# Grouped-query attention: the stacked, turned and copied keys of one key head shared by the two pairs of query heads that read them

## The reference, cut to what matters

```python
q = (h @ Wq).reshape(b, s, H, HD)        # H = 16 query heads, HD = 16
k = (h @ Wk).reshape(b, s, HKV, HD)      # HKV = 4 key heads
v = (h @ Wv).reshape(b, s, HKV, HD)
q = _apply_rope(q, cos, sin)
k = _apply_rope(k, cos, sin)
k = jnp.repeat(k, H // HKV, axis=2)      # each key head serves 4 query heads
v = jnp.repeat(v, H // HKV, axis=2)
scores = jnp.einsum('bqhd,bkhd->bhqk', q, k) / np.sqrt(HD)
scores = jnp.where(causal, scores, finfo.min)
ctx = jnp.einsum('bhqk,bkhd->bqhd', softmax(scores), v)
```

## Time and profile before

| | |
|---|---|
| Time, median of 3 runs | 3239.17 us (3236.78 to 3246.33) |
| The profiled execution's own time | 3255.24 us |
| Its span | 3253.5 us, mean granted clock of PE 0.956 |
| PE busy in the span | 2867.8 us (88%) |
| DVE, ACT, POOL busy | 2160.3, 1658.5, 1425.3 us |
| The grouped-query stage | from about 1526 to about 2208 us of the span |

### The profile page before, as it was taken

One profiled execution on the slowest core, in us unless ns is written; L12 is line 12 of the kernel. 1 busy time (PEld: TensorE's weight loads), 2 busy tenths in 40 slices (PEclk: granted clock), 3 DMA queues, 4 the chain that ended last, 5 costly groups with the idle time before them and its releaser, 6 DMA issues. The chain is left out here.

```text
span 3253.5 us, 61489 instructions
## 1 busy us (share of the span) xinstructions
PE 2867.8 (88%) x21526; PEld 2294.2 (71%) x21526; DVE 2160.3 (66%) x6229; ACT 1658.5 (51%) x3452; POOL 1425.3 (44%) x2037
## 2 busy tenths in 40 slices
PE   3878789999999999978898898898799999999986
PEld 2555578888888888846666666666578888888864
DVE  3777678678768777756777777766644455454576
ACT  1544444444444444446666666665454555555553
POOL 3577742342333243275656666322222222222377
PEclk8877899999999999989999999999899999999998
DMA  2464567678777777622333333210355556555445
GB/s 79 163 223 177 197 238 304 255 269 313 274 273 279 280 269 276 246 33 56 92 92 105 105 99 103 97 65 22 132 209 200 206 205 225 196 214 200 140 98 124
DMA packets 192070, 580.15 MB, mean 178 GB/s; under 512 B 22856, under 2 KB 144656, under 8 KB 157456
## 3 DMA queue, kind: packets, MB, share of 16 engines
q1 hardware_dynamic: 154896, 525.03, 43.7%
q0 software_dynamic: 36864, 51.14, 7.7%
HBM read 450.14 MB, written 125.96 MB: 177 GB/s over the span
## 5 line engine op out<-in xcount | busy, mean ns | idle before, releaser
L1119 POOL TENSOR_TENSOR al<-t,ah 128x512 fp32r<-128x512 f32 x220 | 285.5, 1298 | 992.2 <-ACT ah L1331 992.2
L572 PE MATMUL bank<-masks_bf,ident_bf 128*128 128x128 bf16 (+1 forms) x2304 | 581.4, 252 | 138.2 <-ACT ksT L1413 45.3
L526 PE MATMUL bank<-xh,gu 128*128 128x256 f32 x3520 | 629.3, 285 | 9.7 <-issue 4.9
L1779 DVE TENSOR_REDUCE st<-bank 128x1 f32<-128x512 f32 (+3 forms) x1024 | 422.9, 481 | 218.7 <-PE bank L579 211.3
L1426 ACT ACTIVATE pt<-bank 128x512 f32<-128x512 f32 (+1 forms) x1152 | 513.2, 539 | 105.7 <-PE bank L582 95.6
L572 PEld LDWEIGHTS bank<-masks_bf,ident_bf 128*128 128x128 bf16 x2304 | 225.6, 98 | 425.4 <-issue 98.8
L526 PEld LDWEIGHTS bank<-xh,gu 128*128 128x128 f32 x3520 | 506.0, 191 | 19.5 <-issue 13.3
L582 PE MATMUL bank<-qaT,ksT 128*128 128x512 f32 (+3 forms) x1536 | 443.7, 392 | 0.0
L579 PE MATMUL bank<-ksT,qsT 128*128 128x512 f32 (+3 forms) x1536 | 438.6, 384 | 0.0
L1434 ACT ACTIVATE oT<-bank 128x512 f32<-128x512 f32 x192 | 114.4, 596 | 552.6 <-PE bank L649 519.3
L526 PE MATMUL bank<-xl,gu 128*128 128x256 f32 x1760 | 352.9, 282 | 0.0
(11 more groups left out here) (250 smaller groups left out, 5226.9 us busy)
## 6 DMA issues: line engine op xcount, KB each, us to landing
gu<-wu_scratch SPq DMA_DIRECT2D x110, 2056.0 KB, 8.0
dn<-wd_scratch SPq DMA_DIRECT2D x110, 1024.0 KB, 9.6
xs<-xs_scratch SPq DMA_DIRECT2D x110, 264.0 KB, 9.0
ys_scratch<-yb SPq DMA_DIRECT2D x110, 256.0 KB, 9.9
raw<-in_gu SPq DMA_DIRECT2D x16, 1024.0 KB
wu_scratch<-hi SPq DMA_DIRECT2D x16, 1024.0 KB
wu_scratch<-lo SPq DMA_DIRECT2D x16, 1024.0 KB
xs_scratch<-empty SPq DMA_DIRECT2D x32, 264.0 KB
```

What stands on the lines that cost most here:

```text
L526: mm = pe.matmul(bank[:, TS * h:TS * (h + 1)], gu[:, col:col + P], x[s % 2][:, TS * k:TS * (k + 1)], start=(n == 0), stop=(n == len(terms) ...
L572: pe.matmul(bank[:, diag:diag + P * len(unit)], ident_bf[:, :], masks_bf[:, 0 if which == "q" else 1, 0:len(unit), :].rearrange("p n k -> ...
L1119: pool.tensor_tensor(em["al"][s % 2][:, m, :], em["t"][g % 2][:, :], em["ah"][s % 2][:, m, :].bitcast(F32), ALU.subtract).then_inc(al_read ...
L1779: ins = dve.reduce_max(st[:, 0, r:r + 1], bank[:, first:first + width], AX.X)
```

## The change

Where a unit is "gqa", pair G with odd p no longer stacks, turns or copies keys; it reads those of pair G - 1. Key tiles are counted by key head (`key_at`), so that the two pairs read the same one of the two `ksT` buffers. Before an odd pair's scores PE waits for the copy of its queries alone. POOL has 4 instructions for an odd pair in place of 7. The waits of the ring move with the missing bank. The line on `first_banks` gives another division of banks to the general path, which is taken only if a flag is raised, and which is not in the profile; in the program measured here `first_banks` stays what it was.

```diff
+        def key_pair(G):
+            return G - G % (NP // HKV) if kinds[G // NP] == "gqa" else G
+        key_pairs = sorted({key_pair(G) for G in range(steps)})
+        key_at = {G: key_pairs.index(key_pair(G)) for G in range(steps)}
...
-        first_banks = narrow if 0 in plan else wide
+        first_banks = (banks[0:2], banks[2:8]) if general else wide
...
-                            ks = mem["ksT"][G % 2][j]
+                            ks = mem["ksT"][key_at[G] % 2][j]
...
                     turn_q(f"Tq{G}", G)
+                    if key_pair(G) != G:
+                        return
                     ks = mems[kinds[G // NP]]["kst"]
...
                 def keys_in(G):
-                    pe.wait_ge(x_act, X.count[f"Tk{G}"])
-                    pe.wait_ge(k_half, G + 1)
+                    pe.wait_ge(x_act, X.count[f"Tk{G}" if key_pair(G) == G else f"Tq{G}"])
+                    pe.wait_ge(k_half, key_at[G] + 1)
...
-                    if G >= 1:
-                        pool.wait_ge(x_full, X.full(f"Tk{G - 1}"))
+                    own_keys = key_pair(G) == G
+                    if G >= 1 and own_keys:
+                        pool.wait_ge(x_full, X.full(f"Tk{key_pair(G - 1)}"))
...
                     pool.tensor_copy(qs[:, :, :, 0:HD].bitcast(F32R), q).then_inc(pool_step, 1)
+                    if not own_keys:
+                        chain.n += 1
+                        pool.wait_ge(pool_step, chain.n)
+                        pool.tensor_tensor(qs[:, :, :, HD:2 * HD], q, qs[:, :, :, 0:HD], ALU.subtract).then_inc(pool_step, 1)
+                        pool.memset(qs[:, :, :, SHIFT:SHIFT + 2], 0.0).then_inc(pool_step, 1)
+                        chain.n += 2
+                        pool.wait_ge(pool_step, chain.n)
+                        pool.tensor_copy(qs[:, :, :, 2 * HD:3 * HD], qs[:, :, :, 0:HD]).then_inc(stack_ready, 1)
+                        return
...
                     act.activation(mem["qsT"][:, :], X.bank(f"Tq{G}")[:, :], ACT.Copy).then_inc(x_act, 1)
+                    if key_pair(G) != G:
+                        return
                     act.wait_ge(x_full, X.full(f"Tk{G}"))
-                    bank = X.bank(f"Tk{G}")
-                    act.activation(mem["ksT"][G % 2][0][0:SW, :], bank[0:SW, :], ACT.Copy).then_inc(k_half, 1)
-                    act.activation(mem["ksT"][G % 2][1][SW:P, :], bank[SW:P, :], ACT.Copy).then_inc(x_act, 1)
+                    bank, keys = X.bank(f"Tk{G}"), mem["ksT"][key_at[G] % 2]
+                    act.activation(keys[0][0:SW, :], bank[0:SW, :], ACT.Copy).then_inc(k_half, 1)
+                    act.activation(keys[1][SW:P, :], bank[SW:P, :], ACT.Copy).then_inc(x_act, 1)
```

## The result

The changed kernel takes 3224.44 us (median of 7 runs, 3219.39 to 3231.8). The kernel before, run beside it, takes 3246.89 us (7 runs, 3236.78 to 3250.89). The ratio is 0.9933 with a 95% interval of 0.9921 to 0.9946, so the change takes away 21.8 us (17.5 to 25.6). The forecast was 3223 us and 16.1 us of gain from 3239.17. The time is 1.4 us from the forecast, but part of that is luck: the runs beside it had a slower kernel before than the three runs I started from, so the gain to be explained is 21.8 us and not 16.1. The forecast gain lies just under the interval of the measured one.

A forecast was written before the change was run, and what follows sets the result against it. PE was taken as the bound, with DVE close behind; 6.5 + 0.8 + 3.1 + 7.7 + 0 = 18.1 us, less 2 us for the clock, took 3239.17 to 3223 us (chance 0.62), range 3208 to 3235.

The forecast's parts named there:

- What bounds the stage: Changed stage: PE busy 89%, DVE at 75% close enough to take over in single steps.
- p = 4: Step preparing pair 5: 1.05 us freed, capped by DVE's idle time at 0.81 us; 6.5 us over eight units.
- the second rival: The next steps, p = 5 and p = 7, give the gain back: about 4 us gained, 3235 us; chance 0.18.
- p = 2: Step preparing pair 3: fillers hide ACT's copies, only transposes go; 0.44 us in seven units, 3.1 us, first unit 0.8.
- p = 6: Step preparing pair 7: router filler falls on an older bank, 1.30 us in five units; 7.7 us over all.
- p = 0: Step preparing pair 1: no gain, DVE's maxima bind; wait at fifth bank grows from 1.55 to about 2.6 us.
- The clock: PE's longer wait in p = 0 lowers the granted clock; 2 us lost, net of about 1 regained behind p = 6.
- The Trainium skill's budget for a copy: ACT's key copies: 0.72 us estimated per 512-column copy, freeing 1.4 us instead of 1.05; swallowed by DVE's cap at p = 4, p = 0.
- The first: Rival: DVE caps nothing, all 32 odd pairs gain what PE and ACT are freed of; 29.3 us, 3210 us; chance 0.13.
- The third: Rival: PE falls to the lower clock behind longer waits and thinner steps; slower, 3257 us; chance 0.05.
- The fourth: Rival: pairs still wait for keys of their own, no change of time, 3239 us; chance 0.02.

The follow-up runs named there:

- the experiment with the scatter: Changed kernel with POOL's scatter of step p = 3 moved behind the stacking of pair 6; 3242.54 us, ratio 0.9952 to the kernel before.
- the run that puts the take back: Changed kernel, but the bank ring still turns on by one for an odd pair, as if keys took it; 3257.86 us, ratio 0.9994 to the kernel before.
- after again: The changed kernel unaltered, run once more; 3240.5 us, ratio 0.9942 to the kernel before.
- the kernel with the ten matmuls: Changed kernel with ten unread bf16 matmuls of 512 columns ahead of the fifth bank in p = 0; 3231.14 us, ratio 0.9909 to the kernel before.

## Why the prediction was right, and where not

**What bounds the stage: right.** PE, in single steps DVE. The largest wait named, for the second key copy, is the one that fell (18.9 to 6.2 us).

**p = 4: the amount was right, the route wrong.** The forecast was 0.81 us a unit, 6.5 in all, since DVE's idle time before its maxima was 0.81. The step gained 1.04 in each middle unit (9.26 to 8.22), 8.7 in all eight, the full amount that PE and ACT were freed of. PE, then DVE, in that step after (the view of PE ended at 1730, so it counts three of four projection matmuls):

```profile
1728.32 1.04 PE L507 MATMUL bank<-ident,qst 128*128 128x128 f32 x8
1729.19 1.13 PE L616 MATMUL bank<-w_gqa,xT 128*128 128x384 f32 x3
1730.58 0.23 PE L579 MATMUL bank<-masks_bf,ident_bf 128*128 128x128 bf16 x1
```

```profile
1730.13 1.23 DVE L1965 TENSOR_TENSOR lo<-raw,hi 128x1024 fp32r<-128x1024 f32 x1 [0.46 <-ACT hi L1483]
1731.28 3.27 DVE L1800 TENSOR_REDUCE st<-bank 128x1 f32<-128x512 f32 x8
```

The cap is there: DVE's idle time is gone, and it starts 0.70 us behind the scores in place of 0.55. But a start that is 0.15 us late did not delay PE in this step: there is no wait for DVE at its fifth bank. The claim "if DVE is late, PE is late by the same amount" was the step that failed; here there was slack. Then p = 5 gave back 2.2 us. From the scores of p = 4 to the filler of p = 5 it is 8.89 us, 8.43 before (1752.70 less 1744.27; the row after again stops at the view's end):

```profile
1739.47 0.88 PE L616 MATMUL bank<-w_gqa,xT 128*128 128x384 f32 x2 [1.03 <-DVE both L1887]
```

This is the second rival's loss in the next step, on another route than the one I had judged harmless. POOL's stack moved beside DVE's rotation and made it slow, as the experiment with the scatter shows: with the scatter moved, p = 4 and p = 5 of the third unit together took 18.94 us, against 19.36 after and 19.93 before. The direct wait, PE's turns for POOL, was 1.3 us in 603 (weight loads of PE after, same window as the groups above):

```profile
L507 PEld LDWEIGHTS bank<-ident,qst 128*128 128x128 f32 x464 | 52.9, 140 | 5.7 <-issue 4.4 <-POOL kst L1180 1.3
```

The sum of p = 4 and p = 5, -6.56 us, meets the 6.5 by two errors that cancel, which is luck.

**p = 2: right.** 0.44 us in a middle unit. The sum over the units was 4.6 against 3.9 (with the first unit's 0.8), and the rest is the late ACT in the one execution of before. The first unit's part cannot be judged: its step took 8.20 to 10.00 us in the kernels that share pair 3, and 9.42 to 11.04 in those that do not.

**p = 6: the mechanism was right, the size not.** The term was 7.7 us and 10.1 were measured. The five units with a mark for a wait were to give 1.30 each (6.5) and gave 1.1 to 1.7 (7.3). Of the two without one, the last gave 0.42 (forecast 0.44), but the second gave 1.38. There the one execution of before misled: PE had lost 0.41 us a little earlier in that step to a late exponential of ACT, and so the filler did not wait. In the executions that share pair 1, 3 or 5 alone, the second unit's filler waits 0.72 to 0.75 us like the others. Pair 3 alone, PE:

```profile
1663.30 1.92 PE L707 MATMUL bank<-wr,cT_gqa 128*128 128x8 f32 x16 [0.73 <-DVE both L1887]
```

That is 0.9 of the 2.4 us of difference; the five are 0.8, and the first unit is 0.7. It gave 1.07 in place of 0.37 in p = 6, but DVE's cap, which I had put there, held: it shows one column later, as a wait at the fifth bank, and p = 7 took 0.80 more. PE in p = 6 of the first unit after:

```profile
1590.99 0.23 PE L579 MATMUL bank<-masks_bf,ident_bf 128*128 128x128 bf16 x1 [0.28 <-ACT qsT L1428]
...
1593.17 0.28 PE L579 MATMUL bank<-masks_bf,ident_bf 128*128 128x256 bf16 x1 [0.70 <-DVE st L1800]
```

So this cap was right. p = 6 and p = 7 together gave 10.3 us, 2.6 more than the term: this is the largest excess over the forecast. It is of one execution, too: the repeated changed kernel has 8.6 us here, 0.9 more than the term. That the bank is the cause, as the prediction argued, is shown by the run that puts the take back.

**p = 0: right.** No gain: -9.3 and +11.4 us. The wait was predicted as about 2.6 us and is 2.7 to 3.2 in six units; in the first two it went from 0.2 to 1.3. PE after, in the fourth unit:

```profile
1766.94 0.23 PE L579 MATMUL bank<-masks_bf,ident_bf 128*128 128x128 bf16 x1 [0.28 <-ACT qsT L1428]
```

That is the start of the scores; 4.7 us later comes the matmul with the wait of 3.21 shown above.

**The clock: right in sign, its size not settled.** 2 us were to be lost, and p = 0 and p = 1 lost 2.06. The unit that had escaped went from 20.98 to 22.76 us (+1.8; forecast 1.5), the others changed by -0.3 to +0.4. Two profiled executions can't settle such a sum, though: the kernels that left p = 0 as it was differ from before by -2.4, +3.2 and -2.6 us there (pairs 3, 5 and 7 alone), since it varies which units escape. The five that share pair 1 and add nothing in p = 0 (after, after again, pair 1 alone, the bank put back, the scatter) lie at +0.7 to +2.1. Of the first two units, for which I had counted an even chance of a fall, the second had none. The first had one (0.97 in p = 1, 0.86 in p = 2), but so had the kernel with the ten matmuls (0.99, 0.83), so the wait is not its cause. The falls in p = 7, which I expected to go with the filler's wait, went: two units of before had one (0.85 and 0.82), none after. The granted clock in the fourth unit, from the scores in p = 0 to those in p = 1, is 0.89 over 15.7 us (before 0.88 over 14.0):

```profile
1766.90:1782.60 15.70, 10.87 (x76) 7.60 (x77) 11.64 (x44) 7.14 (x14) 9.41 (x15) 0.89 0.25 60
```

The stage's mean clock did not fall to 0.97 but stayed at 0.98.

**The Trainium skill's budget for a copy.** The Trainium skill ("ScalarE: Activation LUTs", Rules for kernel authors) would have given, as an estimate, 1.4 us for the two copies; the trace has 0.59 us for each, and p = 4 gained 1.04, so the rows' price was the right one. The section states its 0.3 us for an ACTIVATE with its bias in a pointer operand, and the copies are called without a bias, so the budget may not be made for them.

**The rivals.** The first (no cap, 29.3 us) held for p = 4 within the step and fell for p = 0, where the wait took all, and for p = 6 of the first unit. The second (given back) happened in p = 5 alone. The third (clock) is real in p = 0, where pair 1 alone came out at 1.0012 (1.0001 to 1.0023), but the other three pairs outweigh it, and p = 7 got its clock back. The fourth is excluded by the halved counts. In all, the forecast of 18.1 less 2 us stands against 19.75 us of the stage and 21.8 us of the runs. The 2 us between these last two are within the interval; the 3.6 between forecast and stage are p = 6 with p = 7 (2.6) and p = 2 (0.7), and smaller ones. With the repeated changed kernel's stage (656.65 us) the gain is 16.6 us, so most of the 3.6 is within what one execution can tell.

## What to carry to other kernels

When an operation disappears from a ring of banks, ask first what the following operations take: here the bank that one filler takes, in p = 6, was worth 9 of the 21.8 us, and with the old banks put back nothing clear of noise was left of the gain. Do not take an idle time of the second engine as a cap, unless you know which later instruction needs it and how much slack is between. And where a wait for another engine cannot be removed, a few unread matmuls in it may be worth a good part of such a change: 10 us here in the two steps and about 8 in the time, against 21.8 us for the whole sharing of keys.

## What was unexpected

The clock falls behind waits of 1.5 to 3.2 us for DVE, and in p = 7 behind waits of 0.4 to 1.2 us, in a stage in which PE is 89% busy. It does not fall behind every one of them: a unit of before waited 1.59 us in p = 0 and kept 1.00. A fall behind the wait of p = 0 costs 1.5 to 2 us in a middle unit (22.5 to 23.0 against 20.96). It is not only the wait that costs: the work behind it runs slow. A DVE instruction with two inputs of 128x128 took 0.56 us in place of 0.28 while POOL subtracted beside it, and POOL's own casts of 128x128 took 0.30 us (after) or 0.88 (scatter moved), in the second case while DVE was at its maxima, a cause that no run settles:

```profile
1743.67 0.88 POOL L1161 CAST qst<-qk 128x128 fp32r<-128x128 f32 x1
```

An ACT copy of 64 partitions by 512 columns takes 0.59 us, as long as one of 128 partitions within 10% (0.65 us). So halving the partitions of a copy saves nothing to speak of.
